# A decoder layer on one core: a new order of steps on all five engines and a new table of PSUM banks

## What is computed

```python
# block 1: gated linear recurrence over the tokens
q = silu(x @ Wq1 @ Wq2)                       # 256 -> 128 -> 512
a = exp(log_sigmoid(sigmoid(x @ Wk1 @ Wk2)))  # the decay, 512 channels
v = x @ Wv
h[t] = a[t] * h[t-1] + (1 - a[t]) * v[t]
out = q * h
out = out * rsqrt(mean(out * out) + 1e-6) * norm_w
x = layernorm(x + out @ Wo)
# block 2: cross attention, 8 heads that split the 256 tokens into groups of 32;
# scores and softmax run over the 256 channels of x and of ctx
qk = einsum('bdm,bdn->bmn', xh, ctxh) / sqrt(32)
x = layernorm(x + einsum('bmn,bcn->bcm', softmax(qk), ctxh))
# block 3: gated feed-forward, 1024 hidden channels
x = layernorm(x + (silu(x @ w_gate.T) * (x @ w_up.T)) @ w_down.T)
```

## Time and profile before

| | us |
|---|---|
| median of 3 runs | 170.59 (170.33 to 171.08) |
| the profiled execution, device time | 171.22 |
| its span, first to last instruction | 169.4 |
| PE busy | 155.8 (92% of the span) |
| DVE, ACT, POOL busy | 99.2, 97.3, 94.3 |

### The profile page before, as it was taken

How to read it: one execution, slowest core, us unless ns; L and a number is a source line. 1 busy time by engine, 2 the same in 40 slices (tenths; PEclk the granted TensorE clock), 3 DMA queues, 4 the chain that set the end, 5 groups by cost and what they waited for, 6 DMA issues and landing times.

```text
span 169.4 us, 4236 instructions
## 1 busy us (share of the span) xinstructions
PE 155.8 (92%) x1682; PEld 139.3 (82%) x1682; DVE 99.2 (59%) x201; ACT 97.3 (57%) x151; POOL 94.3 (56%) x124
## 2 busy tenths in 40 slices
PE   7899998999699979899999999896999999999970
PEld 5689897988595969798979897764989699999970
DVE  2349659885847895528388538657633492342343
ACT  3397968978589385695713772958248246024400
POOL 3039999899967227366772194382908346125302
PEclk9999999999999999999999999999999999999997
DMA  4979999901020400000001010000000001010001
GB/s 131 314 299 292 344 403 408 400 23 66 0 62 5 122 0 4 0 4 0 4 17 45 6 62 0 4 0 4 0 4 0 6 0 62 0 63 3 0 0 62
DMA packets 6162, 13.63 MB, mean 80 GB/s; under 512 B 768, under 2 KB 2048, under 8 KB 6144
## 3 DMA queue, kind: packets, MB, share of 16 engines
q1 hardware_dynamic: 5280, 10.23, 17.3%
q0 software_dynamic: 864, 3.15, 5.4%
HBM read 12.32 MB, written 1.05 MB: 79 GB/s over the span
## 4 chain that ended last, share of the span: by engine, by line
PE 80%; DVE 5%; POOL 4%; issue 4%; DMA 3%; ACT 1%; SPq 1%; POOLq 0%; DVEq 0%; ACTq 0%
PE banks L435 41%; PE banks L657 9%; PE banks L444 5%; PE banks L662 4%; PE banks L619 4%; PE banks L582 3%; DMA prob<-w 3%; PE banks L554 3%; PE banks L599 2%; PE banks L564 2%; POOL w_gate_lo L1079 1%; DVE banks L949 1%; PE banks L511 1%; PE banks L543 1%; PE banks L576 1%
## 5 line engine op out<-in xcount | busy, mean ns | idle before, releaser
L949 DVE TENSOR_REDUCE banks<-banks 128x4 f32<-128x1024 f32 x16 | 19.7, 1229 | 14.4 <-PE banks L554 11.6
L1144 POOL TENSOR_TENSOR g_lo<-gu,g_hi 128x512 fp32r<-128x512 f32 x15 | 19.2, 1286 | 11.5 <-ACT g_hi L813 11.5
L1106 POOL TENSOR_TENSOR spare<-prob 128x512 f32<-128x512 f32 x12 | 15.3, 1289 | 15.5 <-ACT prob L775 15.5
L805 ACT ACTIVATE gu<-banks 128x512 f32<-128x512 f32 x16 | 9.5, 597 | 24.8 <-PE banks L435 24.7
L994 DVE TENSOR_TENSOR gu<-gu,banks 128x512 f32<-128x512 f32 x16 | 10.8, 680 | 11.1 <-ACT gu L805 10.9
L775 ACT ACTIVATE prob<-banks 128x1024 f32<-128x1024 f32 x16 | 15.6, 1021 | 1.7 <-PE banks L587 1.5
L657 PE MATMUL banks<-w_down_hi,g_hi 128*128 128x256 f32 x64 | 16.2, 285 | 0.0
L657 PE MATMUL banks<-w_down_lo,g_hi 128*128 128x256 f32 x64 | 15.9, 280 | 0.0
L782 ACT ACTIVATE res<-banks,shift,rstd 128x256 f32<-128x256 f32 x16 | 8.2, 560 | 12.2 <-POOL shift L1129 12.2
L435 PE MATMUL banks<-x2t_hi,w_gate_hi 128*128 128x256 f32 x64 | 13.8, 296 | 1.2 <-ACT x2t_hi L796 0.8
L435 PE MATMUL banks<-x2t_lo,w_gate_hi 128*128 128x256 f32 x64 | 13.0, 284 | 0.1
(11 more groups left out here) (147 smaller groups left out, 443.6 us busy)
## 6 DMA issues: line engine op xcount, KB each, us to landing
prob<-w_ffn SPq DMA_DIRECT2D x4, 512.0 KB, 7.3
res<-xT SPq DMA_DIRECT2D x4, 256.0 KB, 5.2
spare<-w_ffn SPq DMA_DIRECT2D x2, 512.0 KB, 6.9
w_gate_hi<-w_ffn POOLq DMA_DIRECT2D x2, 512.0 KB, 4.6
res<-x SPq DMA_DIRECT2D x4, 256.0 KB, 6.5
ctx_t<-ctxT SPq DMA_DIRECT2D x4, 256.0 KB, 4.0
ctx_raw<-ctx SPq DMA_DIRECT2D x4, 256.0 KB, 5.0
w_up_hi<-w_ffn POOLq DMA_DIRECT2D x2, 512.0 KB, 7.5
```

The lines of the kernel that those rows point to most:

```text
L805: nc.scalar.activation(gu[:, n % 2, :].rearrange("p (k t) -> p k t", k=2), place["gate", b, i][:, :, :], ACT.Silu).then_inc(gate_done, 1)
L949: nc.vector.tensor_reduce(neg_top(b, t)[:, 4 * k:4 * k + 4], place["scores", b, i][:, :, :], AX_X, ALU.max, negate=True).then_inc(top_done, 1)
L1106: nc.gpsimd.tensor_tensor(paired[:, 2 * i:2 * i + 2, :], prob[:, 2 * i:2 * i + 2, 0, :], prob[:, 2 * i:2 * i + 2, 1, :], ALU.add).then_inc ...
L1144: nc.gpsimd.tensor_tensor(g[1][:, 2 * i:2 * i + 2, :], gu[:, n % 2, :].rearrange("p (k t) -> p k t", k=2), g[0][:, 2 * i:2 * i + 2, :], AL ...
```

## The change

All numbers of `PLAN` and `BANKS` are replaced; no code is touched. The planner that made them now also counts a delay between full products and those on 32 rows or columns. The same instructions run on each engine, in another order, and the waits for freed banks fall on other pairs of steps. One line of either table:

```diff
-    "pool.cast_ffn": [[8.95, 9.51, 20.96, 21.52, 24.23, 27.42]],
+    "pool.cast_ffn": [[10.7, 17.67, 18.23, 18.79, 30.43, 38.83]],
...
-    "scores": [[0, 4, 2, 4], [6, 2, 4, 2], [2, 0, 4, 0], [0, 6, 2, 6]],
+    "scores": [[4, 0, 4, 2], [0, 4, 4, 0], [2, 4, 0, 6], [0, 2, 4, 2]],
```

More of the change, by code:

```diff
@@ L67 @@
[L67 to L89, removed]
@@ new lines @@
+    "pe.value": [[8.8, 10.51], [21.6, 24.5], [28.49, 30.66], [55.91, 57.36]],
+    "pe.query": [[13.66, 14.51], [23.05, 23.77], [32.76, 33.48], [76.11, 76.84]],
+    "pe.squares": [[17.63], [32.19], [44.25], [87.04]],
+    "pe.mixed": [[18.19], [34.44], [46.25], [95.72]],
+    "pe.scores": [[26.76, 39.97], [55.0, 64.02], [75.2, 91.67], [108.43, 120.37]],
+    "pe.turn_top": [[34.2, 43.92], [58.81, 67.83], [86.21, 95.48], [115.13, 124.18]],
+    "pe.shifted": [[37.43, 44.99], [59.87, 71.05], [87.52, 98.7], [116.19, 125.24]],
@@ new lines @@
+    "pe.sums": [[49.23], [77.65], [105.74], [132.28]],
+    "pe.context": [[50.99], [78.58], [106.67], [133.21]],
+    "pe.turn_x": [[59.34], [86.51], [115.37], [140.84]],
+    "pe.hidden": [[61.04, 64.93, 68.07, 72.21], [88.69, 92.58, 99.86, 102.76], [117.36, 121.29, 126.41, 129.3], [142.21, 145.28, 148.17, 151.06]],
+    "pe.down": [[80.42], [109.35], [135.05], [153.95]],
+    "act.xt": [[], [5.01], [7.59], [35.02]],
+    "act.low": [[6.04, 10.27], [13.33, 17.67], [19.1, 29.88], [45.41, 47.33]],
@@ L145 @@
-    "up": [[0, 1, 0, 7], [4, 6, 7, 3], [3, 4, 6, 3], [6, 0, 5, 4]],
-    "down": [[5], [1], [2], [0, 2]],
+    "low": [[0, 1], [5, 6], [2, 7], [1, 6]],
+    "decay": [[0, 2], [5, 4], [3, 2], [3, 6]],
+    "value": [[3, 4], [5, 2], [3, 6], [3, 6]],
+    "query": [[7, 3], [4, 6], [2, 4], [6, 7]],
+    "squares": [[3], [7], [7], [3]],
+    "mixed": [[7], [0], [0], [0]],
+    "scores": [[4, 0, 4, 2], [0, 4, 4, 0], [2, 4, 0, 6], [0, 2, 4, 2]],
+    "turn_top": [[5, 0], [7, 3], [2, 3], [7, 7]],
+    "shifted": [[2, 6, 4, 2], [0, 4, 2, 6], [4, 0, 2, 4], [2, 4, 4, 2]],
@@ L147 @@
+    "sums": [[1], [0], [0], [2]],
+    "context": [[2], [6], [5], [6]],
+    "turn_x": [[2], [6], [0], [0]],
+    "gate": [[3, 6, 4, 0], [3, 4, 1, 7], [7, 6, 1, 0], [6, 0, 3, 2]],
+    "up": [[7, 2, 5, 1], [2, 5, 6, 4], [1, 0, 6, 7], [7, 2, 4, 5]],
+    "down": [[7], [6], [1], [1, 0]],
 }
```

99 lines of the change are left out of this document (53 added, 46 removed).

## The result

The changed kernel is slower: median 175.53 us (174.68 to 175.81, four executions) against 170.84 (170.33 to 172.74, four), a ratio of 1.025 [1.019, 1.030]. That is +4.7 us; the forecast was +1.5 with an upper end of +3.2. The profiled execution took 175.81, its span is 174.0 against 169.4.

The account below looks back on a forecast made before the run. PE was taken as the bound, busy 155.8 of 169.4 us, with only its standing time able to change. Terms +1.9 +0.9 +0.1 -1.5 +0.1 gave +1.5, so 170.6 + 1.5 = 172.1 us, range 169.2 to 173.8.

Parts of the forecast that it names:

- Term 1: Start to first `scores`: a late cast of chunk 1 holds POOL's root and the norm, +1.9 us.
- Term 2: Second `scores` of batch 0, right behind `shifted`, waits for the first exponential's bank: net +0.9 us.
- Term 3: From there to the first `hidden`: cover for `turn_x` against new waits on POOL and maxima, +0.1 us.
- Term 4: First `hidden` to last `down`: waits removed 3.9 us, waits added 2.4 us, net -1.5 us.
- the changes of form: Tiling-mode changes along PE's order, 42 before and 43 after, about 0.1 us each: +0.1 us at most.
- the end: From the last `down`: the same chain as before, 0.
- rival A: Cast of chunk 1 lands in time, under 5 us: first stretch +0.2, total 170.4 us; chance 0.2 shared with another rival.
- the lower bound: Until the first `scores`, with a cast of 4.4 us: nobody waits for it, but `w_high` lands later, +0.2 us.
- C: POOL falls further behind, casts of 8.1 and 6 us: 174.5 us at worst, 173.5 with one; chance 0.15.
- B: Kernel gets faster: cast in time, earlier `w_high`, late waits covered, 168.8 us; chance 0.15.

Follow-up runs that it names:

- e1: Changed kernel with the cast of chunk 1 issued early again, right behind that of chunk 0: median 170.56 us, ratio 0.996.
- e2: Changed kernel, cast still late, with twelve small identity products ahead of the first `scores`: median 172.90 us, ratio 1.011.
- e3: Kernel before the change with the cast of chunk 1 issued late and its subtraction ahead of the first norm's root: median 174.79 us, ratio 1.015.
- e6: Changed kernel with POOL's subtraction for chunk 1 moved behind the first norm, cast still late: median 171.26 us, ratio 1.000.
- e13: Early-cast kernel (e1) with `mixed` of batch 3 moved back behind `shifted`: median 172.45 us, ratio 1.006.
- the joined orders: Two kernels, e7 and e8, that join stretches of the old and new orders and banks: medians 180.15 and 179.75 us.
- e7: Old order and banks up to `turn_x` of batch 0, the changed kernel's from there: median 180.15 us, ratio 1.049.
- e12: Early-cast kernel (e1) with six identity products ahead of the second `turn_top` only: median 169.94 us, ratio 0.992.
- e9: Early-cast kernel (e1) with five identity products ahead of the first `scores` and six ahead of the second `turn_top`: median 171.25 us, ratio 1.000.
- e8: As e7, but with the changed kernel's start and the early cast up to the first `scores`: median 179.75 us, ratio 1.048.
- e10: The early-cast kernel (e1) run again unchanged: median 170.33 us, ratio 0.997.
- e11: As e2, with four identity products instead of twelve: median 174.72 us, ratio 1.017.
- e4: Changed kernel with `mixed` of batch 1 put back between `shifted` and the second `scores` of batch 0: median 178.43 us, ratio 1.040.

## Why the prediction was wrong

The sign was right, the size was not: 175.5 lies above the upper end of 173.8. Term by term:

| term | forecast | measured | by |
|---|---|---|---|
| 1: until the first `scores` | +1.9 | +2.2 | 30.48 - 28.31 |
| the clock | not in the sum | +2.9 | 16.36 - 13.42 |
| 2: `scores` behind `shifted` | +0.9 | +0.9 | 13.42 - 12.54 |
| 3: until the first `hidden` | +0.1 | +0.2 | moved work taken out |
| 4: until the last `down`, with the changes of form | -1.4 | -1.6 | moved work taken out |
| the end | 0 | 0 | 11.08 - 11.07 |
| sum | +1.5 | +4.6 | |

**The step that failed** is in the first paragraph: "PE's own work stays what it is, and what can change is the time in which PE stands". PE's instructions stay, but their durations hang on the granted clock. A stand of 3.05 us was followed by 6.8 us at 1.2 GHz; at 0.43 per pair where 0.235 is usual, that costs 2.9, more than the stand did. e1 (no stand) and e2 (stand filled, `scores` as late) both keep the clock, and e3 brings the loss up in the old order. Part of the evidence was there to see: the trace before had the column at 1.00 over all its stands, of which the longest is 1.58, it showed 0.50 only from 167.0 on, with PE idle since its last products at 164.2, and my own term 1 made a stand longer than 1.58. The question that I didn't put is how long PE would stand in one piece. The Trainium skill, TensorE: Matmul & The Clock Gate, HAM oscillation — how this bites in real kernels, says that waits for transfers between bursts of matmuls put the array back to its lower clock; the traces here show the same behind shorter waits for other engines, with the stands and stretches listed at the end. With it the forecast would have been 172.1 plus 1.5 to 2.9 (the two lengths measured below), 173.6 to 175.0.

**Term 1** came out well by two errors that cancel in the time of `scores` but not in the stand. I walked the landing of chunk 1 right (26.2; it was 26.3, with 7.9 us for a transfer that I priced at 6.9, issued 0.9 earlier). I walked `w_high` wrong: it landed at 7.4, not 8.4, PE reached `scores` at 27.4 and not 28.5, and so stood 3.05 instead of 1.8. The same error made rival A and the lower bound too dear: with the cast in time term 1 is not +0.2 but -1.1 (27.25 against 28.31), half of it because PE's first products come 0.5 us earlier with `low` of batch 0 fed first.

**Term 2** held: the stand is 1.28, and the net +0.9 is what e1 shows against before. **Term 3** held, and its doubt on POOL's last subtraction was real: 0.40 after the change, 0.65 in e1, 1.83 in e6. **Term 4**: the three stands named as removed are gone, the two named as added are there. The changes of form play no part that I could see; a `hidden` between `shifted` and `scores` takes 3.08 against 2.97 beside another `hidden`. That `mixed` is a cover was shown (e13); for the others I have only the two traces, since the joined orders failed.

**The rivals.** C was nearest with 174.5 "at the worst", but by the wrong mechanism: POOL was no further behind than forecast. (With one of its two late casts C is 172.1 + 1.2 = 173.3, not the 173.5 that I wrote.) B would have needed the cast in time, and e1 shows what that gives: span 167.7, 169.5 to 170.0 us in the faster half of its executions, where I had said 168.8.

## What to carry to other kernels

When a change makes PE wait, add up the stand in one piece and compare it with the longest that the trace shows without a drop of the granted clock. That one is not safe either, as the same 1.58 us kept the clock in the profile of before and lost it in that of e7. Beyond it, price the work behind it at the lower level as well, since that can cost more than the wait. In a queue without reordering, ask of every instruction that waits for a transfer what stands behind it: moving one subtraction behind the norm (e6) was worth 4.8 us with the transfer as late as before. A stand that can't be removed may be filled with products that nobody reads, but only where PE really stands (e12 against e9).

## What the runs showed of the hardware

- Stand of PE, then the stretch at 0.50 behind it, in the profiled executions: 1.58 none (before, after, e1, e3, e6, e8, e13) or 3.4 us (e7); 1.59 none (e2, e10) or 3.4 us (e11); 2.23 (e11) 3.4 us; 2.26 and 2.27 (e4) none; 2.66 (e3) 3.4 us; 3.06 (e4, at its first `scores`) 3.4 us; 3.05 (after) 6.8 us; 3.50 and 3.18 within 5 us (e8) 10.3 us. Between 1.58 and 2.27 us it went both ways, also with the same order of work. What decides it, and the length of the stretch, I did not find.
- 3.4 us at the lower level cost 1.5 (e3, and the second of e11) to 1.8 us (e7), 6.8 cost 2.9. The gap between the two groups of e1 and e10 is about 1.4, and their mean clocks differ by 0.01. That one such stretch makes the gap is supported by e7's profile and by the missing upper group where the 1.58 us stand was filled (e12); no execution of the upper group of e1 or e10 itself was profiled.
- A 512 KB cast issued by POOL took 4.2 to 5.1 us from issue to landing with few of SP's loads outstanding (issued at 11 to 13 us, or alone behind SP's burst) and 5.7 to 11.6 with SP's loads outstanding, the transfers together near 400 GB/s. The Trainium skill, DMA: Bandwidth & Descriptors, Anatomy of one DMA, would give 3.2 as an estimate for the size; no cast here was that short.
